# Polynomial attention: from a second-degree feature map to squared scores, with unused bf16 matmuls beside them

## The reference, cut to what matters

```python
    def _L1_attn_ref(x, Wqkv, bqkv, Wproj, bproj, temperature):
        A, Bc, Cc = (0.5, 1.0, 1.0)
        H = 8
        EPS = 1e-12
        ...
        B, N, C = x.shape
        D = C // H
        scale = float(D) ** 0.25
        qkv = (x @ Wqkv.T + bqkv).reshape(B, N, 3, H, D)
        ...
        q = q * scale
        v1 = jnp.concatenate([jnp.ones((B, H, N, 1), dtype=v.dtype), v], axis=-1)
        qn = _normalize(q) * (scale * temperature)
        kn = _normalize(k) * scale
        vN = v1 / N
        kv_mod = jnp.einsum('bhni,bhnj,bhne->bhije', kn, kn, vN)
        kv = jnp.einsum('bhnd,bhne->bhde', kn, vN)
        vsum = jnp.sum(vN, axis=-2)[:, :, None, :]
        y = A * jnp.einsum('bhni,bhnj,bhije->bhne', qn, qn, kv_mod) + scale ** 2 * Bc * jnp.einsum('bhnd,bhde->bhne', qn, kv) + scale ** 4 * Cc * vsum
        y_norm, y = (y[..., :1], y[..., 1:])
        y = y / y_norm
        out = jnp.transpose(y, (0, 2, 1, 3)).reshape(B, N, H * D)
        return out @ Wproj.T + bproj
```

## Time and profile before

| | us |
|---|---|
| three runs | 1997.10, 1999.03, 2000.07 |
| median | 1999.03 |
| the profiled execution | 2006.71 |
| its span | 2004.9 |
| taylor stage, first VectorE step to last store | 1388.5 to 1714.0 |

### The profile page before, as it was taken

The page is one execution under the profiler, slowest core; times in us unless marked ns, Lnnn a source line. Parts: engine busy times, 40 slices in busy tenths (PEclk is TensorE's granted clock), DMA queues, the critical chain, the costliest instruction groups (busy, mean ns, idle before and its releaser), DMA issues. The chain is left out here.

```text
span 2004.9 us, 45616 instructions
## 1 busy us (share of the span) xinstructions
PE 1719.6 (86%) x15064; PEld 1344.4 (67%) x15064; DVE 1488.5 (74%) x4423; ACT 756.6 (38%) x2274; POOL 690.5 (34%) x957
## 2 busy tenths in 40 slices
PE   1499999999769999999999999973999999788887
PEld 1266666666557777777777777752888888677776
DVE  6166676666627898888889888875766665688887
ACT  2245454545324444344344444321222222343442
POOL 2622222222134555545545445532211111322221
PEclk9999999999869999999999999985555555788788
DMA  2000000000000000000000000000000000000000
GB/s 114 1 2 0 0 0 0 0 0 0 1 1 1 1 2 0 0 0 0 0 0 0 0 0 0 1 1 0 1 0 0 0 0 1 1 5 8 4 6 11
DMA packets 6980, 8.13 MB, mean 4 GB/s; under 512 B 6272, under 2 KB 6272, under 8 KB 6784
## 3 DMA queue, kind: packets, MB, share of 16 engines
q1 hardware_dynamic: 6912, 7.25, 1.1%
HBM read 5.71 MB, written 1.54 MB: 4 GB/s over the span
## 5 line engine op out<-in xcount | busy, mean ns | idle before, releaser
L1142 ACT ACTIVATE ex_pT<-ex_T 128x376 f32<-128x376 f32 (+1 forms) x384 | 162.8, 440 | 217.1 <-PE ex_T L1044 207.9
L604 ACT ACTIVATE al_prob<-al_S,al_negmax 94x94 f32<-94x94 f32 (+1 forms) x512 | 146.2, 375 | 180.0 <-DVE al_negmax L731 180.0
L1207 DVE TENSOR_REDUCE ex_negmax<-ex_R 94x2 bf16<-94x376 f32 (+1 forms) x384 | 186.8, 543 | 30.6 <-PE ex_R L1015 30.0
L1044 PE MATMUL ex_T<-ex_qm,ex_kpad 128*128 128x188 f32 x1024 | 189.7, 329 | 0.0
L505 PE MATMUL al_S<-al_kpad,al_qT 128*94 128x376 f32 x384 | 166.5, 516 | 0.0
L1044 PEld LDWEIGHTS ex_T<-ex_qm,ex_kpad 128*128 128x128 f32 x1024 | 163.0, 192 | 5.1
L944 POOL TENSOR_SCALAR_AFFINE_SELECT ex_pT<-ex_pT 128x512 f32<-128x512 f32 x128 | 84.3, 659 | 236.5 <-ACT ex_pT L1142 236.5
L682 POOL TENSOR_TENSOR al_kpad<-al_kT,al_quad_mask 128x1504 f32<-128x1504 f32 x32 | 86.2, 2692 | 186.3 <-ACTq L619 186.3
L731 DVE TENSOR_REDUCE al_negmax<-al_S 94x2 f32<-94x376 f32 (+1 forms) x192 | 99.1, 542 | 62.6 <-PE al_S L506 56.7
L1554 POOL TENSOR_TENSOR ta_kk<-ta_ext 94x320 f32<-94x320 f32 x64 | 60.4, 961 | 246.4 <-DVE ta_qkn L1734 163.0
L1027 PE MATMUL ex_R<-ex_sxT,wsb 128*128 128x188 f32 x256 | 72.3, 364 | 47.5 <-DVE ex_negmax L1207 47.5
(11 more groups left out here) (308 smaller groups left out, 4300.8 us busy)
## 6 DMA issues: line engine op xcount, KB each, us to landing
tok_xin<-x_t SPq DMA_DIRECT2D x4, 760.0 KB, 6.9
wsb<-weights SPq DMA_DIRECT2D x1, 2531.0 KB, 14.2
out<-stream SPq DMA_DIRECT2D x16, 94.0 KB
tok_par<-tok_w SPq DMA_DIRECT2D x1, 4.5 KB, 1.7
```

The costliest lines, as they stand in the source:

```text
L604: last = nc.scalar.activation(p[:, k, cols], S[0:P, k, cols], ACT.Exp, bias=negmax[g % 2][:, m:m + 1])
L1044: last = nc.tensor.matmul(T[:, k, (j % 2) * N:(j % 2 + 1) * N], kpad[par][:, j, 0:K0], qm[e % 2][:], start=True, stop=True)
L1142: nc.scalar.activation(pT[e % 2][rows, k, cols], T[rows, k, cols], ACT.Exp)\
L1207: red(dst, src, AX.X, ALU.max, negate=True).then_inc(sem["r_used"], 1)
```

## The change

The feature map goes. The new stage (DEPTH 5) forms the scores of each head and squares them:

- q and k are written into blocks padded to 32 per head (`PAD_D`), transposed in eight 128x94 transposes into one bank `QK` (L1610 of the changed kernel), and copied by two ScalarE operations of 128x376 (L1675).
- `scores` (L1536): per row two groups of eight f32 matmuls, each a tile of 32 of the array's rows, `tile_position=(32j, 0)`, into four banks `T`. `kernel_of` (L1642): four ScalarE squares of 94x752 with the bias `linear` (TS2), PSUM to `prob`.
- `weigh` (L1548): per row two groups of eight f32 matmuls in column tiles, values padded to 32 per head. VectorE copies their result, 128x376, to `oT`. Y is formed in the bank `X` by four 94x72 matmuls with `flat_part` (the constant term) and four 94x36 matmuls with `pick` (L1593, L1596).
- `keep_busy` (L1556): bf16 matmuls of 128x512 whose results are overwritten: 18 ahead of row 0's first scores, then in each row one ahead of the q and k transposes and one ahead of the q, k, v projection.
- Biases: `xT` and `yT` get a row of ones and the weights a row of biases, so the additions L1765 and L1772 go; GpSimd keeps only constants, 16 of them. Most tiles have one buffer, and `X` holds xT, yT, Y and the projected row in turn.

The core of the diff, where "..." also stands for the lines taken out (they can be read above):

```diff
-    ("wqkv", 192), ("bqkv", 192), ("wproj", C), ("bproj", C), ("temp", TH),
+    ("wqkv", 192), ("wproj", C), ("temp", TH),
...
-        CONSTS = 22
-        DEPTH = 8
...
+        CONSTS = 16
+        DEPTH = 5
...
         @block.tensor
         def _(pe):
+            def scores(r, g):
+                u = G * r + g
+                if g == 0:
+                    pe.wait_ge(qk_ready, 2 * (r + 1))
+                need(pe, t_used, u)
+                for s in range(HALVES):
+                    for j in range(GH):
+                        rows = slice(32 * j, 32 * j + 32)
+                        last = nc.tensor.matmul(T[0:P, j, s * N:(s + 1) * N], kT[rows, g, s * P:(s + 1) * P],
+                                                qT[rows, g, :], start=True, stop=True, tile_position=(32 * j, 0),
+                                                skip_group_check=True)
+                last.then_inc(t_full, 1)
+
+            def weigh(r, p, g):
+                pe.wait_ge(t_used, G * r + g + 1)
+                if g == 0:
+                    pe.wait_ge(v_ready, r + 1)
+                need(pe, o_ready, r)
+                for s in range(HALVES):
+                    for j in range(GH):
+                        last = nc.tensor.matmul(O[32 * j:32 * j + 32, g * N:(g + 1) * N], v1[p][:, s, GH * g + j, :],
+                                                prob[g][:, j, s * N:(s + 1) * N], start=(s == 0), stop=(s == 1),
+                                                tile_position=(0, 32 * j), skip_group_check=True)
+                last.then_inc(w_full, 1)
+
+            def keep_busy(bank, n):
+
+                for _ in range(n):
+                    nc.tensor.matmul(bank, w_parts[:, 0, 0:128], w_parts[:, 0, 128:640], start=True, stop=True)
...
+                rx, rq, rs, rw, rf = t - 1, t - 2, t - 3, t - 4, t - 5
+                odd = 1 - par
+                if isinstance(rs, int) and rs == 0:
+                    keep_busy(T[:, 0, :], WARM)
+                if valid(rs):
+                    scores(rs, 0)
+                if valid(rx):
+                    pe.wait_ge(xn_ready, rx + 1)
+                    need(pe, stored, rf)
+                    pe.sem_inc(fence, 1)
+                    for h in range(HALVES):
+                        last = nc.tensor.transpose(X[0:C, h * P:(h + 1) * P], xn[:, h, :], ident[0:P, 0:P])
+                    last.then_inc(xT_full, 1)
+                if valid(rw):
+                    weigh(rw, par, 1)
+                if valid(rf):
+                    pe.wait_ge(y_ready, rf + 1)
+                    need(pe, stored, rf)
+                    need(pe, xT_ready, upto(rx + 1))
+                    pe.sem_inc(fence, 1)
+                    for h in range(HALVES):
+                        last = nc.tensor.transpose(X[0:C, N + h * P:N + (h + 1) * P],
+                                                   y[:, h].rearrange("p a b -> p (a b)"), ident[0:P, 0:P])
                     last.then_inc(yT_full, 1)
...
+                if valid(rs):
+                    scores(rs, 1)
+                if valid(rw):
+                    pe.wait_ge(o_ready, rw + 1)
+                    need(pe, yT_ready, rf + 1)
+                    if not valid(rf):
+                        need(pe, xT_ready, upto(rx + 1))
+                    for h in range(HALVES):
+                        Y = X[0:P, h * TH * V1:(h + 1) * TH * V1]
+                        for s in range(HALVES):
+                            nc.tensor.matmul(Y.rearrange("p (a b) -> p a b", a=TH), flat_part[:],
+                                             v1[par][:, s, :, 0:V1], start=(s == 0), stop=False, skip_group_check=True)
+                        for g in range(G):
+                            last = nc.tensor.matmul(Y[:, g * GH * V1:(g + 1) * GH * V1],
+                                                    oT[:, g * N + h * P:g * N + (h + 1) * P],
+                                                    pick[:].rearrange("p a b -> p (a b)"), start=False,
+                                                    stop=(g == G - 1), skip_group_check=True)
                     last.then_inc(y_full, 1)
...
+                if valid(rq):
+                    pe.wait_ge(qkn_ready, rq + 1)
+                    need(pe, qk_ready, 2 * rq)
+                    keep_busy(QK[:], 1)
+                    for full, first in ((qT_full, 0), (kT_full, G)):
+                        if first:
+                            pe.wait_ge(qk_ready, 2 * rq + 1)
+                        for g in range(G):
+                            for h in range(HALVES):
+                                last = nc.tensor.transpose(QK[:, g * N + h * P:g * N + (h + 1) * P],
+                                                           qkn[:, h, first + g, :], ident[0:P, 0:P])
+                        last.then_inc(full, 1)
+                if valid(rf):
+                    pe.wait_ge(yT_ready, rf + 1)
+                    need(pe, y_ready, upto(rw + 1))
+                    for h in range(HALVES):
+                        last = nc.tensor.matmul(X[0:P, 256 + h * C:256 + (h + 1) * C], yT[:, h * P:(h + 1) * P],
+                                                w("wproj", C + 1), start=True, stop=True)
                     last.then_inc(out_full, 1)
...
+                if valid(rs):
+                    weigh(rs, odd, 0)
+                if valid(rx):
+                    pe.wait_ge(xT_ready, rx + 1)
+                    need(pe, v_ready, rx)
+                    need(pe, qkn_ready, rx)
+                    need(pe, squares_ready, rx)
+                    keep_busy(QKV[:], 1)
+                    for h in range(HALVES):
+                        last = nc.tensor.matmul(QKV[0:P, h * 192:(h + 1) * 192], xT[:, h * P:(h + 1) * P],
+                                                w("wqkv", C + 1), start=True, stop=True)
                     last.then_inc(qkv_full, 1)
...
+            def kernel_of(r, g, k):
+                if k == 0:
+                    act.wait_ge(t_full, G * r + g + 1)
+                    need(act, w_full, G * (r - 1) + g + 1)
+                ins = nc.scalar.activation(prob[g][:, 2 * k:2 * k + 2, :], T[0:P, 2 * k:2 * k + 2, 0:HALVES * N],
+                                           ACT.Square, bias=linear[:])
+                if k == 1:
+                    ins.then_inc(t_used, 1)
...
+                rx, rq, rs, rf = t - 1, t - 2, t - 3, t - 5
+                if valid(rs):
+                    kernel_of(rs, 0, 0)
+                if valid(rq):
+                    act.wait_ge(norm2_set, rq + 1)
+                    need(act, qkn_ready, rq)
+                    nc.scalar.activation(norm[:], norm2[:], ACT.Sqrt).then_inc(norm_ready, 1)
+                if valid(rs):
+                    kernel_of(rs, 0, 1)
+                if valid(rx):
+                    act.wait_ge(xT_full, rx + 1)
+                    need(act, qkv_full, rx)
+                    nc.scalar.activation(xT[0:C], X[0:C, 0:N], ACT.Copy).then_inc(xT_ready, 1)
+                if valid(rf):
+                    act.wait_ge(yT_full, rf + 1)
+                    need(act, out_full, rf)
+                    nc.scalar.activation(yT[0:C], X[0:C, N:2 * N], ACT.Copy).then_inc(yT_ready, 1)
+                if valid(rs):
+                    kernel_of(rs, 1, 0)
+                    kernel_of(rs, 1, 1)
+                if valid(t):
+                    act.wait_ge(moments_ready, t + 1)
+                    need(act, rstd_set, t)
+                    nc.scalar.activation(std[:], moments[:, :, 1], ACT.Sqrt).then_inc(std_ready, 1)
+                if valid(rq):
+                    for full, dst in ((qT_full, qT), (kT_full, kT)):
+                        act.wait_ge(full, rq + 1)
+                        nc.scalar.activation(dst[:].rearrange("p g n -> p (g n)"), QK[:, 0:G * N], ACT.Copy)\
+                            .then_inc(qk_ready, 1)
...
+                if valid(rw):
+                    dve.wait_ge(w_full, G * (rw + 1))
+                    need(dve, y_full, rw)
+                    nc.vector.tensor_copy(oT[:], O[:, 0:G * N]).then_inc(o_ready, 1)
+                if valid(t):
+                    dve.wait_ge(std_ready, t + 1)
+                    nc.vector.reciprocal(rstd[:], std[:]).then_inc(rstd_set, 1)
+                    dve.wait_ge(rstd_set, t + 1)
+                    need(dve, xT_full, t)
+                    for h in range(HALVES):
+                        last = nc.vector.tensor_scalar(xn[:, h, :], stream[:, t * HALVES + h, :], moments[:, h, 0:1],
                                                        rstd[:, h:h + 1], ALU.subtract, ALU.mult)
                     last.then_inc(xn_ready, 1)
...
+                if valid(rw):
+                    dve.wait_ge(y_full, rw + 1)
+                    Y = X[0:P, 0:HALVES * TH * V1].rearrange("p (a b c) -> p a b c", a=HALVES, b=TH)
+                    nc.vector.reciprocal(rec[:], Y[:, :, :, TD]).then_inc(rec_set, 1)
+                    dve.wait_ge(rec_set, rw + 1)
```

(39 more changed lines are left out.)

332 lines of the change are left out of this document (75 added, 257 removed).

## The result

The changed kernel takes 2163.5 us (median of four, 2161.6 to 2165.1) against 1998.3 before (median of four): ratio 1.082, 95% interval 1.080 to 1.084. It is 165 us slower, outside the range of 1962 to 2115. Rival 1, with a chance of 0.16, gave 2153. The two traces differ by 154.8 us (spans of 2159.7 and 2004.9), since the profiled execution of the kernel before was its slowest.

A forecast was written before the change was run, and what follows sets the result against it. TensorE at 1.2 GHz was taken to bound the stage. At full clock 13.2 + 3.8 + 280.6 (31 turns of 9.05) + 12 + 1.3 = 310.9 against 325.5; with GpSimd's 0.7, −15.3: 1984 us, range 1962 to 2115.

The forecast's parts named there:

- Rival 1: Changed stage: clock stays at 1.2 GHz, turns of 14.5 us, total about 2153 us; chance 0.16.
- What bounds the kernel: Taylor stage before the change: TensorE bounds it, 95% busy at clock 0.50, with a turn of 9.87 us.
- Everything above assumes the clock at 1.00: Changed stage: the forecast's sum takes TensorE at full clock, where the stage before was granted 0.50.
- breaking-even point: Rival 1's deciding point: the gain of 15.3 us is used up with some 9% of turns at half clock.
- The cycle at full clock: New loop's turn through TensorE, ScalarE and VectorE, scores to next scores: 9.07 us, taken as 9.05.
- likeliest case: Changed stage at full clock with the cycle as summed: 1984 us, bounds given as 1963 to 2003; chance 0.57.
- The square: ScalarE's 94x752 square with bias in the new loop: 0.88 us, bounds 0.79 to 1.01.
- side-by-side row tiles: Scores matmuls: a group's row tiles run together, 0.66 us; rival 3, chance 0.05, had them serial at 2.7 us.
- GpSimd's constants: Set-up ahead of the stage: 16 constants instead of 22, 6.1 us before, some 0.7 us less.
- The extra table load: ScalarE in the changed stage: one more table load, 1.3 us, which may as well be nothing.
- The burst: 18 fillers behind the first q, k, v projections: 7.7 us at half clock, half charged, 3.8 us.
- The rule weighed: Clock-gate rule: a busy TensorE gets full clock, an idle one falls back; the forecast noted the trace disagrees.

The follow-up runs named there:

- late-burst run: Changed kernel with the burst of 18 bf16 matmuls moved from row 0's first scores to the projection of turn 5: 2166.7 us.
- six-filler run: Kernel before, with one 512-column filler ahead of each of TensorE's six steps of a turn and a burst at turn 8: 2049.3 us.

## Why the prediction was wrong

- **What bounds the kernel** held: TensorE at 1.2 GHz. The better half of that reading I did not draw: the old stage had a turn of 7.1 in it, to be had by its clock.
- **The step that failed** is "Everything above assumes the clock at 1.00". I took the fillers and the four tiles side by side for enough, since the alibi and expert stages hold it. The late-burst run shows the loop at 2.4 GHz losing it within 6.8 us. At full clock TensorE waits 1.34 us where at half clock it waits 0.54, and with that wait filled the clock holds. I had that wait in the walk (from 2.85 us TensorE waited for the copy) and counted such waits as cover, not as a risk to the clock. The chance of 0.57 for full clock rested on nothing that a row showed for this loop; 0.16 for rival 1 was far too low.
- **Rival 1's price** was near: 14.5 us per turn against 14.90, 2153 against 2163.5. Its breaking-even point, 9% of the turns at half clock, had said how narrow the forecast's ground was.
- **The cycle at full clock** was mis-sized too: 9.07 against 9.92 (9.84 on average) in the run with five fillers behind weigh 1. The ScalarE and VectorE parts hit (1.99, 1.66 and about 1.24 against 1.27). Scores 0 to its square is 1.05 (0.86 summed), from the end of xT's copy at 1580.12 to the next square 1.54 (1.12), out projection to the next scores 2.19 (2.07) after a hand-over of 0.15 for which I had nothing. So hand-overs between engines, 0.1 to 0.25 each, are most of the gap. With 31 × 0.79 = 24 more (9.84 less 9.05), the forecast would have been about 2008 at full clock: slower than before even then. The runs at full or nearly full clock agree, 2020 and 2023; they also carry a late burst and five or eight more fillers per row.
- **The bounds of the likeliest case** were added up wrongly: 1984 − 11 − 4 and 1984 + 16 + 5 + 4 give 1969 to 2009, not 1963 to 2003.
- **The square** (0.88), side-by-side row tiles, GpSimd's constants (5.3 us, 1380.67 to 1385.95, instead of 6.1: a saving of 0.8 where 0.7 was forecast; the rest of the 2.6 us by which the stage starts earlier lies ahead of them) and a filler as 0.43 at half clock (0.40 measured) were right. The extra table load, 1.3 in the sum, wasn't there: both stages have one.
- **The burst** was charged 3.8 and cost about 2 in the stage, its 10.2 us at full clock counted in.
- **The rule weighed**: the Trainium skill, TensorE: Matmul & The Clock Gate, Part 1, says a TensorE that keeps busy is released to full clock. If busy means the profile's busy share, the traces disagree in three kernels: 95%, 92% and 99% busy at 0.50. Its other half, that one that idles falls back, fits what the late-burst run did behind its wait of 1.34 us. But idling is not the whole of it either: the six-filler run fell behind narrow matmuls, with its last wait, 0.49 us, 5.8 us back.

Still open: what exactly of TensorE's work the clock goes by. In the changed loop the runs show that fillers in the waits keep it, that the same number in a lump doesn't, and that busy time doesn't either; they don't tell rows, columns and types apart. In the old loop place and amount changed together. Not tried: the changed loop with its fillers and no burst at all, and a shorter cycle for it.

## What to carry to other kernels

Look at the granted clock of a stage before its busy shares: a stage at 1.2 GHz and 95% busy has up to half its TensorE time to gain, and a new algorithm judged at full clock may well be run at half. To hold the clock, find the waits and the narrow matmuls of a turn as it is at full clock (not the ones that show at half clock) and fill those; the same number of fillers in a lump cost 101 us more here. A burst isn't needed where the fillers are right: in both loops they raised the clock by themselves. What the trace shows just before the clock falls hints at where a filler is missing. And compare two algorithms at the same clock: with fillers and nearly all of the stage at 2.4 GHz, the old one takes 1924 us here and the new one about 2020. Last, when a single run differs by a few microseconds, look at the stage that was changed before you name a cause.
